# Two score groups and two weighted sums in a row on TensorE, in a four-layer attention and expert kernel

## What is computed

```
q = (x @ Wq + bq).reshape(B, N, H, hd).transpose(0, 2, 1, 3)          # H = 16 heads, hd = 8
kv = (y @ Wkv + bkv).reshape(B2, N2, 2, H, hd).transpose(0, 3, 2, 1, 4)
k, v = (kv[:, :, 0], kv[:, :, 1])
attn = jnp.einsum('bhnd,bhmd->bhnm', q * scaling, k)                  # m = 1601 keys
attn = jax.nn.softmax(attn, axis=-1)
out = jnp.einsum('bhnm,bhmd->bhnd', attn, v)
out = out.transpose(0, 2, 1, 3).reshape(B, N, C)
return out @ Wo + bo
```

## Time and profile before

| | us |
|---|---|
| median of 3 runs | 1853.64 (1852.64 to 1859.54) |
| profiled execution, its own time | 1856.58 |
| its span, first to last instruction | 1854.6 |
| PE busy | 1582.5 (85%) |
| mean granted TensorE clock | 0.92 of full speed |

### The profile page before, as it was taken

The page is one execution under the profiler, slowest core; times in us unless marked ns, Lnnn a source line. Parts: engine busy times, 40 slices in busy tenths (PEclk is TensorE's granted clock), DMA queues, the critical chain, the costliest instruction groups (busy, mean ns, idle before and its releaser), DMA issues.

```text
span 1854.6 us, 34408 instructions
## 1 busy us (share of the span) xinstructions
PE 1582.5 (85%) x12939; PEld 869.8 (47%) x13006; DVE 1103.3 (59%) x2509; ACT 805.9 (43%) x1214; POOL 738.4 (40%) x1145
## 2 busy tenths in 40 slices
PE   3289798889988898889998898889988798899667
PEld 3133363346633574336633574345733465347425
DVE  3276476546766576556766476655766477655323
ACT  2146426651366425671366524661266524672211
POOL 0336305741178214771168313771058412750140
PEclk8589799988999999999999999997999999999757
DMA  6310300022000300012000200012000200000000
GB/s 196 64 39 28 89 1 1 27 48 46 1 10 19 67 26 1 18 38 50 15 10 20 67 26 1 18 34 44 26 1 28 56 15 1 2 14 4 1 0 3
DMA packets 64853, 53.65 MB, mean 29 GB/s; under 512 B 14762, under 2 KB 57140, under 8 KB 64692
## 3 DMA queue, kind: packets, MB, share of 16 engines
q1 hardware_dynamic: 64692, 51.47, 11.4%
HBM read 38.98 MB, written 12.46 MB: 28 GB/s over the span
## 4 chain that ended last, share of the span: by engine, by line
PE 63%; DVE 10%; POOL 10%; ACT 5%; issue 5%; SPq 4%; DMA 3%; POOLq 0%; ACTq 0%; DVEq 0%
PE um L671 12%; PE um L660 9%; PE ob L604 8%; PE um L661 7%; PE um L576 5%; DVE mx L1022 4%; PE um L591 4%; POOL big L1236 3%; PE um L554 3%; DMA kst<-k_parts 2%; DVE mx L1127 2%; ACT probs L846 2%; PE um L645 2%; SPq L498 1%; PE um L712 1%
## 5 line engine op out<-in xcount | busy, mean ns | idle before, releaser
L1022 DVE TENSOR_REDUCE mx<-um 128x2 f32<-128x802 f32 (+1 forms) x512 | 504.9, 991 | 228.4 <-PE um L576 220.9
L846 ACT ACTIVATE probs<-um 128x1024 f32<-128x1024 f32 (+1 forms) x448 | 426.6, 963 | 228.0 <-PE um L591 221.6
L852 ACT ACTIVATE hid<-um 128x256 f32<-128x256 f32 (+3 forms) x328 | 125.5, 383 | 503.7 <-PE um L661 503.6
L604 PE MATMUL ob<-probs,vaug 128*9 128x256 f32 (+1 forms) x3328 | 286.9, 394 | 12.4 <-ACT oT L822 12.2
L1201 POOL TENSOR_TENSOR big<-iotab,idx_lo 128x512 bf16<-128x512 bf16 x256 | 266.0, 1055 | 14.7 <-PE um L748 9.5
L576 PE MATMUL um<-kst,qa 64*128 64x401 bf16 (+1 forms) x1024 | 184.2, 359 | 63.6 <-DMA kst<-k_parts 38.1
L1164 POOL CAST qst<-nm 128x4 bf16<-128x4 f32 x64 | 17.1, 268 | 470.9 <-DVE nm L1028 470.4
L591 PE MATMUL um<-big,kst 64*128 64x256 bf16 (+1 forms) x1664 | 173.0, 281 | 16.5 <-ACT big L892 4.6
L1040 DVE SCALAR_TENSOR_TENSOR x<-um,cw,x 128x128 f32<-128x128 f32 x288 | 87.7, 346 | 126.2 <-PE um L671 126.2
L1034 DVE TENSOR_TENSOR hid<-hid,um 128x256 f32<-128x256 f32 (+3 forms) x328 | 133.5, 412 | 24.2 <-ACT hid L852 22.8
L576 PEld LDWEIGHTS um<-kst,qa 64*128 64x128 bf16 x1024 | 50.1, 95 | 202.3 <-issue 65.8
(11 more groups left out here) (209 smaller groups left out, 2265.1 us busy)
## 6 DMA issues: line engine op xcount, KB each, us to landing
kst<-k_parts SPq DMA_DIRECT2D x384, 50.0 KB
k_parts<-big SPq DMA_DIRECT2D x72, 128.0 KB, 1.9
ctx_sb<-in_ctx SPq DMA_DIRECT2D x8, 768.0 KB
k1st<-k_parts SPq DMA_DIRECT2D x96, 32.0 KB
k_parts<-big SPq DMA_DIRECT2D x24, 64.0 KB, 1.6
kst<-in_L_ffn_w SPq DMA_DIRECT2D x1, 1408.0 KB
x<-in_x SPq DMA_DIRECT2D x8, 128.0 KB, 2.2
out<-x SPq DMA_DIRECT2D x8, 128.0 KB, 1.9
```

The lines of the kernel that those rows point to most:

```text
L604: m = pe.matmul(ob[q:q + V1, 0:NQ], vaug[b % 2][0:kn, c, 2 * p + hh, :], probs[0:kn, (2 * (NGB * b + g) + hh) % NPS, (c % 2) * NQ:(c % 2 + ...
L846: act.activation(probs[0:kn, k:k + 2, 0:w], own_banks, ACT.Exp).then_inc(f_read, 1)
L852: act.activation(hid[0:nr, own % NHID, :], quarter[place[ev][0]][0:nr, 0:NQ], ACT.Silu).then_inc(th_ready, 1)
L1022: dve.tensor_reduce(mx[:, p % 2, s, :, j], pair[:, :, 0:w], AX, ALU.max, negate=True).then_inc(u_read, 1)
```

## The change

Two numbers of the table change. Groups with an odd number in the sequence (0 to 55) are put 0.9 units earlier, their scores and their weighted sum, so that they stand right behind those of the even group before.

```diff
                 for g in range(NGB):
-                    put(own + g, "s0", b, g)
-                    put(own + g + 2.3, "w0", b, g)
+                    put(own + g - 0.9 * (g % 2), "s0", b, g)
+                    put(own + g - 0.9 * (g % 2) + 2.3, "w0", b, g)
```

## The result

| | before | changed |
|---|---|---|
| median | 1856.59 us | 1955.03 us |
| ratio | | 1.0507 (95% interval 1.0409 to 1.0605) |
| profiled execution | 1856.58 us | 1963.13 us |
| mean granted TensorE clock | 0.920 | 0.875 |

A forecast was written before the change was run, and what follows sets the result against it. The prediction took TensorE, busy 85% of the span, to carry the kernel. Its terms, - 24 + 41.6 - 4 + 16 - 8 = + 21.6 us, gave 1875 us against the median 1853.64, range 1843 to 1906.

The forecast's parts named there:

- What the change removes: TensorE in the eight layer 0 stages: fewer changes of matmul tile shape, taking 24 us off (15 to 31).
- rival 3: Two weighted sums behind each other still pay 0.12 us for leaving column tiles: + 18 us, 1893; chance 0.06.
- A wait for oT at every second boundary: Four head-pair boundaries a stage: the next pair's sum waits for ScalarE's later copy oT, adding 41.6 us (29 to 47).
- the place worked out: Groups 20 and 21 of one sequence, where a pair reaches over a head-pair boundary: 1.2 us lost.
- The 4 us for groups 41 and 42: TensorE's 1.32 us standstill there is partly filled by other scores: 0.5 us a stage, 4 us, come back.
- PSUM banks: A pair of score groups takes four of seven banks at once, so TensorE waits for releases: 16 us added.
- Banks and clock: Bank waits at their upper bound, or TensorE's clock falling after longer stops, + 24 us for either: 1899; chance 0.12.
- rival 4: The forecast's case of bank waits at their upper bound or a falling TensorE clock: 1899 us; chance 0.12.
- What the stops give back: While TensorE stops, the other engines catch up, so its later waits shrink: 1 us a stage, 8 us off.
- the first sum: The forecast's total over shape changes, oT waits, groups 41 and 42, banks and catching up: + 21.6 us.

The follow-up runs named there:

- the filled kernel: The change, with seven idle matmuls before each of the 32 weighted sums that wait for oT, eleven at a stage's last boundary: 1912.13 us, 1.0352 of before.
- both cures: The change, with four groups in the weights' ring, experts' ring of 6, and stops filled with seven or eleven idle matmuls: 1886.99 us, 1.0181 of before.

## Why the prediction was wrong, by its own steps

**"What the change removes", 24 us: right for each change of shape; the total was not measured by itself.** Two scores and two sums cost what was worked out, and rival 3 (column tiles keep their 0.12) fell: 0.98 us for two sums.

**"A wait for oT at every second boundary", 41.6 us: right in mechanism and in size.** The wait list has 62.5 us in 39 places, for the 40 to 60 in over 30 expected; the place worked out takes 2.15 us for 2.25. Which part of the time it made is less clear than that: putting the copy first, 37 us of this wait less, gave 30 us; leaving the sum apart, 29 less, gave 16 by the medians and 5 by the ratios. The 4 us for groups 41 and 42 are in line with the trace, where the stop of 1.32 us there is 0.63 long in five of the stages.

**"PSUM banks", 16 us: of the right size, as far as the waits tell.** The scores (L591) waited 13.1 us for DVE's maxima and ACT's L892 before, and 35.8 in the change, 22.7 more or 2.8 a stage.

**The term that was left out: the ring of weights.** The sum of the prediction has no term for an exponential that waits for a weighted sum: it stands there at nothing, without a reason. In the place that I worked out the last sum follows right behind the two scores and ends at +1.15, before the second exponential can start at +1.35, so the wait is covered there. But every second exponential of a pair now needs a sum that PE issues only behind both score groups, where it was issued between them before, and elsewhere in the stage other work stands ahead of that sum as well. ScalarE is idle then, 121 us in 161 places, and a ring of four, which takes this wait away, gave 49 us back (45 by the ratios), 29 of 43 in the profiled executions as busy time of PE. That ScalarE is busy for only 43% of the span made it look harmless; but a share of busy time says nothing about an order in which every second operation is late.

**"Banks and clock", 24 us for either and a chance of 0.12: the mechanism was right, its size was not.** I expected one more stretch at the lower clock a stage, at 3 us. There were 193 us more at the lower clock in the run, 24 us a stage, and filling the stops gave back 43 us (29 by the ratios). That PE stops four more times a stage, for 1.3 to 2.5 us, was in the forecast; that the clock falls behind most of these stops is in no row that I had read. The trace of the kernel before shows it, though: its only stops for oT of this length are the seven of 1.32 us at groups 41 and 42, and behind three of them, those that end at 381.76, 1020.95 and 1229.05, the clock is down within three us. Three of seven, for 32 new stops, would have given rival 4 a far larger price. The Trainium skill, "TensorE: Matmul & The Clock Gate", section "HAM oscillation", names this kind of failure, idle time between bursts that sends the clock down again and again. Here the trace agrees in kind, with stops of 1.3 to 2.5 us and a mean clock of 0.875; the case worked there has longer stops, waits for a DMA, so it gives no price for these.

**"What the stops give back", 8 us: too small.** PE waits 50 us more for oT and 23 more for banks, and its idle time grew by 41 at most, so its other waits shrank by 30 us or more. Nearly all of that is the wait for the load of keys ahead of the stages, which fell from 38.1 to 8.7 us; in the filled kernel it is at 23.9 us again, so part of what the clock took was given back this way and is no gain.

**What is left once clock and ring are out.** With both cures 32 us are left (22 to 45), for 21.6 forecast from shape changes, stops and banks. That is near, but no proof of the first sum: the idle matmuls are in those 32, mostly in time in which PE would have waited, and two of its terms of opposite sign, banks and what the stops give back, were both too small.

**Open.** What the *sums* in pairs cost. Alone they lose 1.1%, in spite of 189 fewer shape changes; with a ring of four, both in pairs is 15 us behind the scores alone. It isn't the ring, since with the sums alone in pairs exponentials wait 0.5 us for a sum in the whole run, and the clock is only a little lower, 0.917. The planner may give the banks in another order there, and I ran nothing that holds it fixed.

## What to carry to other kernels

Grouping like matmuls saved about 0.1 us here for each change of tile shape, but it pays only if the buffers behind them can hold the longer bursts: count, for each ring, how many producers now stand ahead of the consumer that frees a slot, and don't let a group reach over a point where an accumulator is handed over. Price every new regular stop of TensorE twice, once as a wait and once for the lower clock behind it; a split into busy and idle time of the span shows at once which of them a slower kernel has.

## What was not expected of the hardware

The clock fell behind 27 of 32 stops of only 1.3 to 2.5 us, in a kernel whose TensorE is busy 85% of the span. Between the change and the kernel with filled stops, PE's busy time without the idle matmuls differs by 1659.0 - 1578 = 81 us and the time at the lower clock by 490 - 290 = 200: 0.4 us for each us at the lower level. Idle matmuls put in front of a wait made this kernel faster: 256 of them, by 43 us (29 by the ratios).
